# Rotation of k shared with GpSimd, and five waits and places moved, in a fused cross-attention and quantised feed-forward kernel

## The reference, cut to what matters

```python
x = x + xattn(layernorm(x), ctx, ctx, wq, wk, wv, wo, wo_b)     # x, ctx: (16, 256, 512) f32
x = x + ffn(layernorm(x), W_in, b_in, W_out, b_out)             # 512 -> 2048 -> 512

# xattn: qp = rope(q @ wq.T); kp = rope(k @ wk.T); vp = v @ wv.T    16 heads of 32
#   rope(x) = concat(x1*cos - x2*sin, x1*sin + x2*cos), x1 and x2 the halves of the 512 columns
#   scores = qh @ kh.T * sqrt(32), only |query - key| <= 128 kept; softmax; @ vh; @ wo.T + wo_b
# ffn: weights fake-quantised to 8 bits by row or column, x and hidden to 16 bits by one global
#   maximum each; hidden = gelu(x @ W_in + b_in), out = hidden @ W_out + b_out
```

## Time and profile before

| | |
|---|---|
| median of 3 runs | 1233.8 us (1231.41 to 1234.8) |
| the profiled execution | 1233.87 us, its span 1232.2 us |
| PE, DVE, ACT, POOL busy | 1148.4, 984.4, 640.7, 367.7 us |
| granted TensorE clock, mean | 0.985 of full speed |
| a step of stage A | 43.6 to 44.4 us |

### The profile page before, as it was taken

How to read it: one execution, slowest core, us unless ns; L and a number is a source line. 1 busy time by engine, 2 the same in 40 slices (tenths; PEclk the granted TensorE clock), 3 DMA queues, 4 the chain that set the end, 5 groups by cost and what they waited for, 6 DMA issues and landing times.

```text
span 1232.2 us, 23572 instructions
## 1 busy us (share of the span) xinstructions
PE 1148.4 (93%) x7884; PEld 770.6 (63%) x7928; DVE 984.4 (80%) x2541; ACT 640.7 (52%) x1001; POOL 367.7 (30%) x540
## 2 busy tenths in 40 slices
PE   6989999999999999999999767999999989999998
PEld 6867777876787787687677545444444444444443
DVE  6868889989888988988988746666666688888886
ACT  5254355345335434534533433655556457777775
POOL 1135346345434624634553331000000030121230
PEclk9989999999999999999999969999999999999999
DMA  8463574565466456457545622555554400677762
GB/s 270 124 143 108 162 180 128 143 176 146 126 176 159 121 151 180 131 141 193 132 122 142 180 82 77 175 207 202 203 195 145 150 4 30 186 223 236 239 223 95
DMA packets 95916, 191.12 MB, mean 155 GB/s; under 512 B 13377, under 2 KB 24769, under 8 KB 95809
## 3 DMA queue, kind: packets, MB, share of 16 engines
q1 hardware_dynamic: 95808, 189.75, 52.2%
HBM read 89.16 MB, written 43.91 MB: 108 GB/s over the span
## 4 chain that ended last, share of the span: by engine, by line
DVE 35%; PE 35%; issue 24%; DMA 2%; ACT 1%; SPq 1%; POOL 0%; DVEq 0%; POOLq 0%; ACTq 0%
PE bank L857 17%; DVE bank L1191 7%; PE bank L521 4%; PE bank L522 4%; PE bank L523 4%; DVE bn L1137 3%; DVE roped L1217 2%; DVE rt L1214 2%; PE bank L604 2%; DVE rt L1215 2%; DVE row_max L1191 2%; DVE neg_max L1232 2%; DVE x_res L1184 2%; PE bank L533 1%; DVE nt_t L292 1%
## 5 line engine op out<-in xcount | busy, mean ns | idle before, releaser
L1191 DVE CUSTOM_DVE_ANT_0 bank<-bank,mask 128x256 f32<-128x256 f32 x512 | 201.6, 455 | 52.1 <-PE bank L604 45.3
L857 PE MATMUL bank<-wout_int,g_lo 128*128 128x512 bf16 x512 | 193.5, 379 | 1.1
L857 PE MATMUL bank<-wout_int,g_hi 128*128 128x512 bf16 x491 | 185.7, 379 | 4.3 <-DVE g_lo L1483 4.0
L818 PE MATMUL bank<-qT_lo,win_int 128*128 128x512 bf16 x496 | 188.0, 379 | 1.2
L818 PE MATMUL bank<-qT_hi,win_int 128*128 128x512 bf16 x474 | 179.6, 379 | 0.0
L960 ACT ACTIVATE probs<-bank 128x512 f32<-128x512 f32 x256 | 142.9, 603 | 50.4 <-PE bank L638 46.1
L1528 POOL TENSOR_SCALAR_AFFINE_SELECT probs<-probs 128x256 f32<-128x256 f32 x256 | 109.9, 433 | 82.8 <-ACT probs L960 79.1
L1483 DVE TENSOR_TENSOR g_lo<-h_int,g_hi 128x512 f16<-128x512 f32 x128 | 104.2, 814 | 34.4 <-ACT g_hi L1100 34.0
L604 PE MATMUL bank<-k_st,q_st 96*128 96x256 f32 x512 | 97.7, 303 | 22.6 <-DVE row_max L1191 20.9
L1521 POOL TENSOR_TENSOR x_res<-x_res,wo_b 128x512 f32<-128x512 f32 x32 | 42.0, 1334 | 237.6 <-DMA x_res<-in_x 230.2
L638 PEld LDWEIGHTS bank<-q_st,k_st 128*128 128x128 f32 x512 | 91.2, 194 | 31.0 <-issue 13.6
(11 more groups left out here) (170 smaller groups left out, 2712.9 us busy)
## 6 DMA issues: line engine op xcount, KB each, us to landing
hidden_scratch<-h_ring SPq DMA_DIRECT2D x96, 256.0 KB, 2.0
h_ring<-hidden_scratch SPq DMA_DIRECT2D x96, 256.0 KB, 2.9
k_st<-k_hi SPq DMA_DIRECT2D x128, 128.0 KB, 2.6
q_st<-q_hi SPq DMA_DIRECT2D x128, 128.0 KB, 2.4
xq<-x_scratch SPq DMA_DIRECT2D x16, 1024.0 KB, 6.1
x_ln<-in_x SPq DMA_DIRECT2D x16, 512.0 KB, 4.6
ctx_raw<-in_ctxT SPq DMA_DIRECT2D x16, 512.0 KB, 5.0
k_st<-k_lo SPq DMA_DIRECT2D x64, 128.0 KB, 2.8
```

What stands on the lines that cost most here:

```text
L818: mm = pe.matmul(bank[f % 4][:], win_int[:, c, f * P:(f + 1) * P], part[:, par, c], start=c == 0 and part is qT_hi, stop=c == KC - 1 and p ...
L857: return pe.matmul(bank[4 * par + u][:], part[:, f % 4, u * P:(u + 1) * P], wout_int[:, f], start=f == 0 and part is g_hi, stop=f == FC - ...
L1191: dve.tensor_tensor_reduce(sc, sc, mask[:, (1 - qb) * P:(1 - qb) * P + S], 1.0, NEG, ALU.add, ALU.max, row_max[:, qb, n:n + 1]).then_inc(m ...
```

## The change

```diff
 def stack_max(b):                                            # SP
-    sp.wait_ge(mT_done, MAX_COPIES * (b + 1))
+    sp.wait_ge(mT_done, MAX_COPIES * b + 1)
     for i in range(1, NC4):
         sp.dma_start(q_st[MROW:P, KC * i:KC * (i + 1)].bitcast(F32),
-                     q_st[MROW:P, 0:KC].bitcast(F32)).then_inc(max_stacked[i - 1], 16)
+                     q_st[MROW:P, 0:1].bitcast(F32).to_broadcast([P - MROW, KC, S])).then_inc(max_stacked[i - 1], 16)
```

```diff
 def x_transposes(j, s):                                      # PE
     if s == 0:
         pe.wait_ge(ln1_norm, 2 * j + 2)
         wait(pe, wt_done, j - 1)
+        wait(pe, rope_step["q"], ROPE_OPS * j)
+    else:
         wait(pe, den_done, j - 1)
-        wait(pe, rope_step["q"], ROPE_OPS * j)
```

```diff
 # ACT, step
-                    if n == 4 and has_proj:
+                    if n == 6 and has_proj:
                         split_hi("q", b + 1)
-                    if n == 8 and has_xt:
+                    if n == 9 and has_xt:
                         ctx_hi(b + 2)
 # DVE, rotate
                     elif not first:
+                        dve.wait_ge(rope_step["k"], ROPE_OPS * (j + 1))
                         dve.wait_ge(lo_done["k"], KC * (j + 1))
+                elif which == "k" and not first:
+                    dve.wait_ge(s, base)
                 dve.tensor_tensor(rt[:, 0], a, (cos, sin)[half], ALU.mult).then_inc(s, 1)
                 dve.tensor_tensor(rt[:, 1], b, (sin, cos)[half], ALU.mult).then_inc(s, 1)
+                if which == "k" and not first:
+                    return
 # POOL, new
+            def rotate_k(j, half):
+                pool.wait_ge(rope_step["k"], ROPE_OPS * j + 3 * half + 2)
+                pool.tensor_tensor(roped[:, 2 * half:2 * half + 2], rt[:, 0], rt[:, 1],
+                                   (ALU.subtract, ALU.add)[half]).then_inc(rope_step["k"], 1)
 # POOL, step: ahead of bias_x, and later low parts
+                if has_proj:
+                    rotate_k(b + 1, 0)
+                    rotate_k(b + 1, 1)
...
-                    if 4 <= n < 8 and has_proj:
-                        split_lo("q", b + 1, n - 4)
-                    if n in (8, 9, 10, 11) and has_xt:
-                        ctx_lo(b + 2, n - 8)
+                    if 6 <= n < 10 and has_proj:
+                        split_lo("q", b + 1, n - 6)
+                    if 10 <= n < 14 and has_xt:
+                        ctx_lo(b + 2, n - 10)
 # POOL, bias_tile (stage C)
                 for u in range(SUB):
+                    pool.wait_ge(hint_done, FC * i + 6 + 2 * u)
                     pool.tensor_tensor(xq[:, par, u], xq[:, par, u], b_out[:], ALU.add).then_inc(xc_b, 1)
```

## The result

| | before | after |
|---|---|---|
| median of 5 runs | 1233.29 us (1231.41 to 1234.8) | 1241.14 us (1239.6 to 1243.47) |
| profiled execution, its span | 1233.87, 1232.2 us | 1241.14, 1238.7 us |
| ratio after to before | | 1.0061 [1.0044, 1.0079] |

The change makes the kernel slower by 0.6%. 1238.7 us was forecast, with 1225 to 1245 as the range.

The account below looks back on a forecast made before the run. A step is bound by PE up to head 10, then by DVE without slack. 13.5 steps of +0.66 us (+8.9), step 0 -0.7, last step +0.5, stage C -3.9: +4.8 on 1233.9, 1238.7 us; 80% range 1225 to 1245.

Parts of the forecast that it names:

- k's additions: Moved from DVE to POOL: -0.23 us a step, but k's low parts then collide with `normalise`, +0.85 us a step.
- The transposes: Parting the inverse from PE's first four transposes, those of s = 0, saves 0.41 us a step.
- The later parts: q's and the context's parts later: POOL slows ln1's tiny DVE instructions, +0.45 us a step (-0.1 to 0.9).
- One length of step: Sign in stage A: late steps fall back to the short length (-0.23 us), so all last near 44.3 us.
- Step 0: Start of stage A: PE's first clump no longer waits for exponential 5; 0.7 us gained (0 to 1.2).
- theory 2: The experiments' rival, no chance given: POOL's late band for PE's last clump causes the loss, long DVE instructions a symptom.
- The last step and the end of stage A: SP's queue runs later by q's low parts, +0.5 us (0 to 0.8), besides half a step.
- Stage C: One POOL addition every two chunks lets DVE keep up; PE's idle time goes, -3.9 us (2 to 4).
- (a): Rival, chance 0.20: no collision that counts in `normalise`; a step -0.54 us, in all 1222.5 us.
- (b): Rival, chance 0.24: gain and loss cancel, one instruction of `normalise` waits (0.57 us); a step +0.13 us, 1231.6 us.
- (d): Rival, chance 0.08: SP's queue is late, `normalise` waits for the shares in six late steps, up to 0.7 us; 1243.
- (c): Rival, chance 0.06: each `normalise` pays 1.13 us and W_in's casts collide too (0.9); a step +1.39, 1248.6 us.

Follow-up runs that it names:

- the version with a step of 43.51: The changed kernel with POOL's second bias addition to x_res held until the split of the maxima (L1199): 1224.15 us, 0.9934.
- the fastest version: The changed kernel with q's and the context's parts at their old places and POOL's second bias addition behind the maxima: 1216.4 us, 0.9875.
- the run with stage C alone: The kernel before with only POOL's output bias in stage C held to every second chunk: 1227.87 us, 0.9969.

## Why the prediction was right, and where it was not

**The loop** held in before and in after. The step is PE up to head 10, then DVE without a gap, and every price followed from the side of head 10 on which the work lay. PE's idle 1.13 us before the last clump, where 0.32 had stood, costs nothing in a steady step; the version with a step of 43.51 has it too. But with the transposes parted and the parts at their old places PE comes up level with DVE. In the fastest version PE's first four transposes start 1.38 us after the inverse (at 256.74), for 0.70 in after, and run straight into the other four; and the chain now passes ACT's cast of q and exponential 5 before the first clump:
```profile
258.12 1.09 PE L534 MATMUL bank<-ident,x_ln 128*128 128x128 f32 x8
...
283.64 1.04 ACT q_hi L907
284.67 0.51 ACT probs L961
```
So the waits that cost nothing in before have no slack left there, and less work for DVE alone should win little more; no run tried it.

**k's additions** were worth nothing on DVE and cost what they pushed. The collision is in thirteen of thirteen steps, at 1.04 us for the 0.85 taken; my clock's own value of 0.97 was nearer than the mean over all phases. A phase that an order fixes is not random from step to step, so averaging over phases was the wrong move. The Trainium skill (SBUF — State Buffer, "Who interferes with whom") has whoever issues first hold the shared port pair for its whole instruction. By the prediction's estimate that gives 1.2, and the trace stands between, since DVE's second instruction again gets going some 0.14 us ahead of POOL's recorded end.

**The transposes** were under-priced: 0.41 forecast, 0.57 measured alone and 0.62 in after (means from the inverse to `normalise`, 17.74 to 17.17 and to 17.12). In all steps of after but the first, where PE comes late out of step 0, 0.61 is there when the next product starts (2.83 to 2.22): the four transposes account for 0.41, and the term left out is PE's restart, 0.26 us behind the end of the inverse before (261.58 + 1.75 to 263.59) and 0.06 after. Four of the thirteen steps win another 0.14 up to head 10, which was not traced further. That `idle before the transposes gone` would show the step right was a poor sign: 0.51 us of it is there, but behind the first four.

**The later parts**: 0.45 forecast, 0.5 measured in steps without a fall of the clock, but partly by luck. ln1's tiny instructions and the copies beside them cost about 0.8 where 0.47 was taken, and W_in's first cast gave 0.3 back; the prediction had named that cast as a possible loss of up to 0.5, and of gains only 0.1.

**One length of step**: most are 44.42 to 44.58 (44.3 was forecast), the first is 44.78, and two in which the clock fell are 45.38 and 45.07; these two gave back half of the -0.23 for the late steps. The size of that term was right, at about -0.2, but its reason was not. In before the stretch from the inverse to `normalise` is 17.70 to 17.80 us in late steps too: the drawn-out addition (1.47 us at 581.25 in the step of the earlier trace rows) did not lengthen it. It made ACT's high part of k late, and with it POOL's low parts, and these ran into `normalise`, 1.46 us in the mean for 1.29.

A step was thus forecast at -0.41 - 0.23 + 0.85 + 0.45 = +0.66, and came out as -0.62 - 0.20 + 1.04 + 0.50 and 0.12 for the two falls of the clock, +0.84. (Means over thirteen steps: inverse to `normalise` 17.74 to 17.12, the pair 1.46 to 2.33, negated maxima to ln1's end 16.71 to 17.30.)

**Step 0** cannot be read from one pair of executions: against the start of the run with stage C alone it is +0.3, where -0.7 was taken. All thirteen profiles say more. From the first row maxima to the first inverse the six kernels with the later parts take 43.3 to 44.4 us (mean 43.71), the seven with the old places 43.8 to 44.7 (44.31): -0.6, near the forecast. PE's first clump comes 0.9 us sooner in all six (28.1 to 28.4 us behind the first row maxima for 28.8 to 29.5), as the wait for exponential 5 went, and 0.3 of it is lost again up to the last clump. There the chain runs through PE's last clump, as in no later step, and what that waits for now is POOL: its last bands stand behind a context low part, as the prediction had named ("POOL's low parts become the next thing late"). The chain of after:
```profile
78.76 0.41 POOL probs L1539
79.17 0.69 POOL cT_lo L1522
79.86 0.73 POOL probs L1539 x2
80.59 0.04 issue
80.64 1.07 PE bank L653 x16
```
So theory 2's mechanism is at work in this one step, for 1.14 us of PE's idle time, and in none of the thirteen behind it.

**The last step and the end of stage A**: +0.8 forecast with the half step, +1.6 measured against before, +3.2 against the run with stage C alone. As these two have the same code there and differ by 1.6, only the sign is sure. By all thirteen profiles the two steps behind the thirteen take 1.0 us more with the later parts (88.6 for 87.6 in the mean, with a spread of some 4 us in each group).

**Stage C**: -3.9 forecast, -4.7 measured. PE's idle time before L858 falls from 4.3 to 0.4 us, which is the 3.9; the other 0.8 was not traced. DVE keeps up:
```profile
1018.77 1.66 DVE L1489 TENSOR_TENSOR g_lo<-h_int,g_hi 128x512 f16<-128x512 f32 x1
...
1020.74 0.68 DVE L1489 TENSOR_TENSOR g_lo<-h_int,g_hi 128x512 f16<-128x512 f32 x1
1021.35 1.49 DVE L1465 TENSOR_SCALAR h_int<-h_int,wout_man 128x512 f32<-128x512 f32 x1
```
Each of POOL's additions holds one instruction of DVE, a low part (1.66 for 0.69) or a rounding to whole numbers (1.49 for 0.49), and the next chunk is free, in place of the 1.76 in turns of the earlier trace rows.

**The sum**: +12.5 for the steps and the end of stage A where +9.4 was forecast, about -0.6 for -0.7 in step 0, -4.7 for -3.9: +7.2 for +4.8, and +7.85 between the medians. The time of 1241.1 lies inside the forecast's own 1236 to 1243. The mechanism held, the main cost came out 0.2 us a step dearer and the main gain 0.2 larger, so the errors of these two cancelled.

**The rivals.** (a) and (b) need a `normalise` that pays little; it pays 1.04 in every step. (d) did not come, but narrowly: in the step shown SP issues the shares at 275.95 and they land 0.36 us ahead of `normalise`, in the narrowest step 0.22. (c), both collisions at full price, would have been 1248.6; it did not come either, since `normalise` pays 1.04 for 1.13 and W_in's casts got shorter. The run with the low parts held back is as slow (1249.7), but by another second meeting, with the negated maxima.

## What to carry to other kernels

Before work is moved to GpSimd, find on VectorE's timeline the point behind which it has no slack, and lay GpSimd's whole queue against it: not the moved instructions but those behind them can decide the price. Here four of 0.7 us, pushed onto one pair, made the same move cost 0.61 us a step where it gains 0.13 with POOL's other work held out of the way. A GpSimd instruction that isn't urgent can be held by a wait until VectorE is past its chain of short dependent instructions; a move without such a wait may only move the collision. And two single executions are poor scales for a stage: a third kernel that shares the stage showed that most of 2.3 us at the start belonged to no edit.

## What the runs showed of the hardware

- A tiny VectorE instruction can wait as long as a large one: 128x32 elements took 1.13 us for 0.19 beside a GpSimd addition of 1.30 us.
- A VectorE instruction with one input in PSUM and one in SBUF did not wait: 128x512 elements took 0.68 us inside a GpSimd addition of 1.29 us.
- The granted TensorE clock fell for some us in one to five of the thirteen steps of seven kernels (clock 0.74 and 0.72 as the mean of 6 us in after, so part at 2.4 and part at 1.2 GHz), in the middle of the step, from 1.1 us ahead of the negated maxima to 1.8 us behind them; such steps last 44.5 to 45.9 us. After, in the step from 396.58, columns as above:
```profile
414.00:420.00 6.00, 4.25 (x19) 2.73 (x19) 5.93 (x21) 1.62 (x3) 3.90 (x4) 0.98 0.00 0
420.00:426.00 6.00, 6.00 (x27) 5.15 (x27) 4.99 (x9) 3.87 (x7) 1.92 (x4) 0.74 0.32 73
```
  PE was busy for 4.25 of the 6 us ahead of it. In the profiled executions the six kernels with a mean step of up to 43.81 us, the kernel before among them, show no such step; the seven from 44.04 on all do. Why some long steps have it and their neighbours don't was not settled.
